# Places of edge groups in a sort block: the segment compare turned so that segments lie on partitions, and the sum moved to the matmul engine

## The reference: what is computed

```python
xn = layernorm(x)
h = xn @ W.T + b;  a1, a2 = h @ w_a1.T, h @ w_a2.T
v = leaky_relu(a1[src] + a2[dst])                 # one value an edge
att = exp(v - segment_max(v, src)) / segment_sum  # softmax over the edges of a node
x = x + segment_sum(att * h[dst], src) + linear_attention(xn)
x = x + slice_attention(layernorm(x))             # 8 heads, 64 slices
```

## Time and profile before

| | |
|---|---|
| median of 3 runs | 1682.46 us (1680.82 to 1684.41) |
| the profiled execution's own time | 1682.33 us |
| its span, first to last instruction | 1680.6 us |
| busy over the span | PE 83%, DVE 78%, POOL 66%, ACT 40% |
| mean granted TensorE clock | 0.914 of full speed |
| loop over the 14 blocks of the sort, on DVE | 79 to 366 us |
| last scatter of the sort, on POOL | 384.1 us |

### The profile page before, as it was taken

The page is one execution under the profiler, slowest core; times in us unless marked ns, Lnnn a source line. Parts: engine busy times, 40 slices in busy tenths (PEclk is TensorE's granted clock), DMA queues, the critical chain, the costliest instruction groups (busy, mean ns, idle before and its releaser), DMA issues. The chain is left out here.

```text
span 1680.6 us, 27556 instructions
## 1 busy us (share of the span) xinstructions
PE 1391.1 (83%) x8473; PEld 1102.6 (66%) x8473; DVE 1310.9 (78%) x3978; ACT 665.2 (40%) x1867; POOL 1111.6 (66%) x1196
## 2 busy tenths in 40 slices
PE   5399989984788889888888888888989888886798
PEld 3277767763567777766666666666767666664587
DVE  8999879973588887888888888888787887873244
ACT  0144333420455454555455454455454544531000
POOL 1078888886777777777777777777777777720000
PEclk9699999985799998999999899899998999997599
DMA  9011112113444444444444444444444444512722
GB/s 231 9 58 53 43 41 65 48 37 87 118 124 123 123 125 124 123 123 127 119 123 123 118 122 123 123 122 124 124 121 124 121 121 116 150 51 68 267 74 72
DMA packets 106322, 180.11 MB, mean 107 GB/s; under 512 B 29183, under 2 KB 77694, under 8 KB 106175
## 3 DMA queue, kind: packets, MB, share of 16 engines
q0 software_dynamic: 44384, 113.26, 26.0%
q1 hardware_dynamic: 48277, 44.22, 9.4%
q10 hardware_dynamic: 13514, 20.87, 3.5%
HBM read 142.98 MB, written 35.29 MB: 106 GB/s over the span
## 5 line engine op out<-in xcount | busy, mean ns | idle before, releaser
L1043 POOL DMA_INDIRECT big<-node_table,rest x850 | 826.6, 972 | 245.4 <-issue 231.9
L1114 PE MATMUL psum<-big 128*125 128x257 f32 x1700 | 437.2, 415 | 73.7 <-DVE big L1615 73.7
L1114 PEld LDWEIGHTS psum<-big 128*125 128x125 f32 x1700 | 342.9, 207 | 139.6 <-DVE big L1615 80.5
L1262 ACT ACTIVATE rest<-big,rest 128x125 f32<-128x125 bf16 x850 | 268.3, 490 | 165.8 <-DVE rest L1563 164.7
L1615 DVE TENSOR_SCALAR big<-big,rest 128x125 f32<-128x125 bf16 x850 | 172.8, 293 | 0.0
L327 POOL DMA_INDIRECT edge_groups<-rest x112 | 143.9, 1285 | 27.2 <-issue 21.8
L1570 DVE TENSOR_REDUCE rest<-rest 128x125 f32<-128x2125 f32 x50 | 118.3, 2367 | 32.2 <-ACT rest L1262 32.2
L1253 ACT COPY big<-psum 125x1024 bf16<-125x1024 bf16 x150 | 103.8, 763 | 38.4 <-PE psum L1091 38.4
L1149 PE MATMUL psum<-big 125*128 125x256 f32 x416 | 101.1, 387 | 0.0
L1135 PE MATMUL psum<-rest,big 128*125 128x512 f32 x208 | 99.7, 601 | 0.0
L1759 PE MATMUL psum<-rest,big 128*125 128x256 f32 x400 | 88.7, 384 | 2.0 <-DVE rest L1812 2.0
(11 more groups left out here) (390 smaller groups left out, 2655.0 us busy)
## 6 DMA issues: line engine op xcount, KB each, us to landing
big<-node_table,rest POOLq DMA_INDIRECT x850
slice_weights<-rest ACTq DMA_DIRECT2D x52, 252.0 KB
big<-slice_weights SPq DMA_DIRECT2D x25, 252.0 KB, 7.4
big<-slice_weights ACTq DMA_DIRECT2D x25, 252.0 KB, 6.9
node_table<-big SPq DMA_DIRECT2D x50, 126.0 KB
normalised_turned<-big SPq DMA_DIRECT2D x50, 125.0 KB
rest<-normalised_turned SPq DMA_DIRECT2D x50, 125.0 KB, 2.5
out_dram<-rest SPq DMA_DIRECT2D x50, 125.0 KB
```

What stands on the lines that cost most here:

```text
L1043: pool.indirect_dma_start(Gt[:, u, q * TW:(q + 1) * TW], None, table, bass.IndirectOffsetOnAxis(ap=item[:, u, 2 * q:2 * q + 1], axis=0)).t ...
L1114: mm = pe.matmul(bank[bAgg][0:R, 0:D + 1], P[:, u, q, :], Gt[:, u, q * TW:q * TW + D + 1], start=q == 0, stop=q == Q - 1)
L1262: act.activation(V[:, :, q], O[:, u, q, 0:R], ACT.Copy, scale=score[:, u, q:q + 1]).then_inc(s_v, 1)
```

## The change

The compare is turned around. The 51 entries now lie on partitions, and the 1024 group numbers along the free axis.

- Once, ahead of the loop: PE transposes the two halves of `starts` (`turn_starts`), ACT copies each block's origins and jumps out of PSUM as columns of 51 partitions, and POOL makes the row of group numbers (an iota of 512 int32 on 51 partitions and its copy to f16), shifts the origins for the second half of the numbers, and splits the jumps into two bf16 parts.
- For each block: DVE compares the 512 numbers of each half with that block's origin of the partition (`groups_reached`, two `tensor_scalar` with f16 in and bf16 out, 51 x 512, the origin being a column operand). It does so one block ahead, and for block 0 just before its first `choose`.
- PE multiplies: for each of the 8 columns of groups, the 51 x 128 piece of the compare is the weight and the two jump parts are the moving columns (`group_jumps`, 8 bf16 matmuls of 2 columns). That gives 128 x 8 x 2 in PSUM.
- DVE adds the two parts (`tensor_reduce`, 128 x 16 out of PSUM), and the old last addition to int32 stays.

`group_jumps(n+1)` stands where `block_starts(n+1)` stood in PE's queue; `group_jumps(0)` stands behind `ranks(3)`, ahead of the loop. Tensors of the first stage are laid over each other in another way to make room.

```diff
+                    pool.iota(group_row_i, [[1, GC * 64]], base=0, channel_multiplier=0).then_inc(masks, 1)
+                    pool.wait_ge(masks, 9)
+                    pool.wait_ge(table_ready, 1)
+                    pool.tensor_copy(group_row, group_row_i).then_inc(masks, 1)
+                    pool.wait_ge(table_part, 6)
+                    pool.tensor_scalar(start_col[:, 1, :], start_col[:, 0, :], -GC * 64.0, None, ALU.add).then_inc(masks, 1)
+                    pool.tensor_copy(jump_parts[:, :, 0], jump_col).then_inc(masks, 1)
+                    pool.wait_ge(masks, 12)
+                    pool.tensor_tensor(jump_parts[:, :, 1], jump_col, jump_parts[:, :, 0], ALU.subtract).then_inc(masks, 1)
...
-                    def block_starts(n):
-                        at = STARTS_AT + 2 * (T + 1) * (n % 2)
-                        pe.matmul(bank[1][:, at:at + 2 * (T + 1)], ident[0:NS, SPB * n:SPB * n + 1].to_broadcast([NS, 128]),
-                                  starts.rearrange("s a t -> s (a t)"), start=True, stop=True).then_inc(starts_psum, 1)
+                    def turn_starts():
+                        pe.transpose(bank[1][0:T + 1, TURNED_AT:TURNED_AT + NS], starts[:, 0, :], ident[0:NS, 0:NS])
+                        pe.transpose(bank[1][0:T + 1, TURNED_AT + NS:TURNED_AT + 2 * NS], starts[:, 1, :], ident[0:NS, 0:NS]
+                                     ).then_inc(starts_psum, 1)
+
+                    def group_jumps(n):
+                        at = STARTS_AT + 2 * GC * (n % 2)
+                        pe.wait_ge(segs, max(3 * n + 1, 2))
+                        for c in range(GC):
+                            mm = pe.matmul(bank[1][:, at + 2 * c:at + 2 * c + 2], reached[:, c // 4, c % 4 * 128:(c % 4 + 1) * 128],
+                                           jump_parts[:, n, :], start=True, stop=True)
+                        mm.then_inc(starts_psum, 1)
...
                     for g in range(2, GPB):
                         ranks(g)
+                    pe.wait_ge(masks, 13)
+                    group_jumps(0)
...
+                    act.wait_ge(starts_psum, 1)
+                    act.copy(start_col[:, 0, :], by_block[:, 0, :, 0]).then_inc(table_part, 1)
+                    act.copy(jump_col, by_block[:, 1, :, 0]).then_inc(table_part, 1)
...
+                    def groups_reached(k):
+                        for h in range(2):
+                            dve.tensor_scalar(reached[:, h, :], group_row, start_col[:, h, k:k + 1], None, ALU.is_ge
+                                              ).then_inc(segs, 1)
...
-                        dve.wait_ge(starts_psum, k + 1)
+                        dve.wait_ge(starts_psum, k + 2)
+                        if k + 1 < NB:
+                            groups_reached(k + 1)
...
-                        dve.tensor_tensor(seg, bank[1][:, at:at + w].unsqueeze(1).to_broadcast([128, GC, w]),
-                                          group_id.unsqueeze(2).to_broadcast([128, GC, w]), ALU.is_le).then_inc(segs, 1)
-                        dve.wait_ge(segs, 3 * k + 1)
-                        dve.tensor_tensor(seg, seg, bank[1][:, at + w:at + 2 * w].unsqueeze(1).to_broadcast([128, GC, w]),
-                                          ALU.mult).then_inc(segs, 1)
-                        dve.wait_ge(segs, 3 * k + 2)
-                        dve.tensor_reduce(seg_sum, seg, AX, ALU.add).then_inc(segs, 1)
-                        dve.wait_ge(segs, 3 * k + 3)
+                        dve.tensor_reduce(seg_sum, bank[1][:, at:at + 2 * GC].rearrange("p (c w) -> p c w", w=2), AX,
+                                          ALU.add).then_inc(segs, 1)
+                        dve.wait_ge(segs, min(3 * k + 5, 3 * NB))
                         dve.tensor_tensor(slot_buf[:, u], seg_sum, group_id, ALU.add).then_inc(slots_ready, 1)
...
                     normalisers()
+                    dve.wait_ge(masks, 13)
+                    groups_reached(0)
                     for g in range(GPB):
                         choose(g)
```

More of the change, by code:

```diff
@@ L142, in bass_gps @@
             key_iota = a.take(128, 128, dtype=F16)
-            iota_i = a.take(128, 128, dtype=I32)
             group_id = a.take(128, GC)
@@ L151, in bass_gps @@
             scal = a.take(1, 4)
-            before = a.take(128, 128)
+            before_at = a.at
+            before, iota_i = a.take(128, 128), a.take(128, 128, dtype=I32)
+            group_row = Arena(rest, before_at, a.at).take(T + 1, GC * 64, dtype=F16)
             item_cmp, item_col = a.take(128, T), a.take(128, 1)
@@ L162, in bass_gps @@
             v2i, v2h = a.take(128, 64, dtype=I32), a.take(128, 64, dtype=I32)
-            seg = a.take(128, GC, T + 1)
+            reached_at = a.at
+            reached = a.take(T + 1, 2, GC * 64, dtype=BF16)
+            group_row_i = Arena(rest, reached_at, a.at).take(T + 1, GC * 64, dtype=I32)
+            start_col, jump_col = a.take(T + 1, 2, NB), a.take(T + 1, NB)
+            jump_parts = a.take(T + 1, NB, 2, dtype=BF16)
             seg_sum = a.take(128, GC)
@@ L199, in bass_gps @@
             hot_done, counted, summed = sem("hot_done"), sem("counted"), sem("block_sums")
-            masks, coded, csum_made, first_made = sem("masks"), sem("coded"), sem("csum_made"), sem("first_made")
+            masks, coded, csum_made, first_made = sem("masks_and_columns"), sem("coded"), sem("csum_made"), sem("first_made")
             table_part, offsets_made, table_ready, starts_psum = sem("table_part"), sem("offsets_made"), sem("table_ready"), sem("starts_psum")
@@ L219, in bass_gps @@
             wa, gb, ba = b.take(128, DC, 2), b.take(128, DC), b.take(128, 2)
-            STARTS_AT, ROW_STEPS = 256, 10
+            TURNED_AT, STARTS_AT, ROW_STEPS = 256, 384, 10
             UNITS = [[] for _ in range(NB)]
@@ L494, in _ @@
                     pe.wait_ge(table_ready, 1)
-                    block_starts(0)
+                    turn_starts()
                     items()
@@ L507, in _ @@
                             pe.wait_ge(moved_made, 3 * (2 * n + 1))
-                            block_starts(n + 1)
+                            group_jumps(n + 1)
                         put(n, 0)
@@ L567, in _ @@
                     assert len(loads) == 12
+                    by_block = bank[1][0:T + 1, TURNED_AT:TURNED_AT + 2 * NS].rearrange("t (a b s) -> t a b s", a=2, s=SPB)
+                    act.wait_ge(starts_psum, 1)
+                    act.copy(start_col[:, 0, :], by_block[:, 0, :, 0]).then_inc(table_part, 1)
+                    act.copy(jump_col, by_block[:, 1, :, 0]).then_inc(table_part, 1)
                     act.wait_ge(prep_psum, 2)
@@ L760, in unpack @@
                         dve.tensor_tensor(edge_buf[:, u, :, 0], v2h, bank[1][:, 128 * h:128 * h + 64], ALU.add).then_inc(edges_ready, 1)
+                    def groups_reached(k):
+                        for h in range(2):
+                            dve.tensor_scalar(reached[:, h, :], group_row, start_col[:, h, k:k + 1], None, ALU.is_ge
+                                              ).then_inc(segs, 1)
                     def places_of_groups(k):
-                        u, at = k % SLOTS, STARTS_AT + 2 * (T + 1) * (k % 2)
-                        w = T + 1
-                        dve.wait_ge(starts_psum, k + 1)
+                        u, at = k % SLOTS, STARTS_AT + 2 * GC * (k % 2)
+                        dve.wait_ge(starts_psum, k + 2)
+                        if k + 1 < NB:
+                            groups_reached(k + 1)
                         if k >= SLOTS:
```

## The result

The changed kernel takes 1672.95 us in the median (1666.29 to 1674.01, 6 runs), the kernel before beside it 1683.6 (1680.82 to 1687.12, 6 runs). The ratio is 0.9934 (0.9916 to 0.9953): 11 us faster, where I had forecast no change and a range from 1675 up. The profiled execution took 1674.01 us, its span is 1672.2.

What follows compares the result with a forecast made beforehand. The prediction took POOL's unbroken queue to bound the sort. From the profiled 1682.3 us, -0.4 for the loop's start and +1.8 for the lock gave 1683.7, forecast as 1683.5, range 1675 to 1687.5.

Steps and rivals of the forecast that it cites:

- Nothing moves in the other stages: Outside the sort's stage: the change was to alter no time there, as no DMA is added.
- Its 71 us of excess stay: POOL in the sort: 71 of 282 us lost beside DVE's f16 operations were to remain, those operations being as many.
- rival B: POOL in the sort: 5 to 10% of the 71 us excess goes, 3.5 to 7 us, giving 1677; chance 0.10.
- The start of the loop: First compare +0.55 us on DVE, block 0 then gains 0.9; POOL's unbroken queue begins earlier, net -0.4 us.
- my lower bound: DVE's new compares: 0.30 us each for 512 elements, at twice the pace of f32.
- my 0.6 to 1.0: DVE's step in each block: the us it was to gain from the change.
- 8 to 13: DVE's two waits for others in the sort, 12.8 us before, were to rise by this many us.
- The lock: DVE's new compares shutting POOL out: 0.15 us for each of twelve pairs, +1.8 us.
- Rival A: DVE sets the sort's pace after all, so its saved time counts: 11 us less, 1671; chance 0.17.
- the last line of my sum: Whole kernel: 1682.3 - 0.4 + 1.8 = 1683.7, that execution 0.1 us below the runs' median; forecast 1683.5.

Runs made afterwards that it cites:

- e_one_cast: The kernel before with one more instruction on POOL, a cast of 128 x 8 int32 to f16 into scratch, without a wait: ratio 0.9965 (0.9951 to 0.9978).
- e_prep_dve: The changed kernel with POOL's new instructions, all but the iota, moved to DVE ahead of its loop: ratio 0.9989 (0.9977 to 1.0001), median 1680.31 us.
- e_more_dve: The changed kernel with three more DVE operations a block (compare, multiplication, reduce of 408 elements, into scratch): ratio 0.9976 (0.9965 to 0.9988).

## Why the prediction was wrong

*"Nothing moves in the other stages"* is the step that failed, and the larger part of the 11 us. Each gather became 7 to 9 ns shorter, 6 to 8 us in 850 of them, and each scatter 9 to 10 ns at its shortest, 1 us in 112. I had counted POOL's five new instructions as run with POOL idle, costing nothing; they didn't cost but paid, through what comes long after them. Shown by `e_one_cast` (5.9 us from one cast alone) and, in the shortest gather and the time, by `e_prep_dve`. No row of the kernel before could have told it. But the earlier trace rows did say that anything that touches the 850 gathers back to back counts in full, and I asked only what was added to them.

*"Its 71 us of excess stay"* failed too. POOL's unbroken stretch, with the same instructions in it, is 4 us shorter on the mean of the four traces with the new step (3.8 in the first pair, 6.0 in the second). The number of f16 operations had stayed, as I said; what POOL lost beside them had not. That is rival B, given 0.10, at the lower end of its 3.5 to 7 us. Half of it went to the later start: 2 us are left at the last scatter, and by `e_prep_dve` some 2 us in the time.

*The start of the loop* was forecast 0.4 us earlier and came later. In the timelines POOL's wait for unit 4 ends at 105.51 us in the changed kernel and at 103.61 in the kernel before:

```profile
105.51 1.36 POOL L353 TENSOR_TENSOR big<-rest 125x256 f32<-125x256 f32 x1 [4.96 <-ACT rest L627]
```

```profile
103.61 1.91 POOL L339 TENSOR_TENSOR big<-rest 125x256 f32<-125x256 f32 x1 [4.97 <-ACT rest L598]
```

The wait is still 4.96 us long, so it hid nothing of PE's delay: units 0 to 3 stand in PE's queue ahead of `put(0, 1)` and unit 4, and whatever delays them delays it. Of the 1.9 us, 0.53 are the first pair, 0.44 `group_jumps(0)` in PE's queue, and 0.7 come from elsewhere: DVE waited for x before its statistics, 1.80 us in the first trace of the changed kernel and 0.73 in this one.

```profile
47.41 16.43 DVE L837 BATCH_NORM_STATS2 rest<-X 125x6 f32<-125x256 f32 x50 [0.73 <-DMA X<-in_x_dram]
```

All seven traces with the new step have such a wait, of 0.5 to 1.8 us, and two of the 13 with the old one; why is open. DVE, level with the kernel before at its first f16 operation (82.29 against 82.20), then waited 2.27 us in block 1, by the order of the queues for the put that stood behind those units; the view names no releaser. POOL's unbroken stretch is 274.6 us against 280.5 in this pair; the gain at the end is 1.9 less than that.

*What held.* The pair, undisturbed, ran at my lower bound, 0.30 us each, which is where the Trainium skill's "VectorE: DVE Perf Modes", section "The perf-mode tier table", puts a 16-bit `tensor_scalar` in SBUF; the trace agrees. The step saved 1.1 us in block 0 and some 0.7 on the mean, within my 0.6 to 1.0; POOL waited for nobody in the loop; DVE's waits rose, by 5 us in the first pair of traces and 4 in the second, not 8 to 13; the first trace's last scatter was within 3 us. The lock has a price, of 0.2 to 0.3 us a pair by estimate, in place of 0.15. The Trainium skill's rule of the shared port pair ("SBUF — State Buffer", section "Who interferes with whom") names who locks out whom, and that agrees with it in kind. By the same rule DVE operations with at most one input in SBUF, outside the 2-port modes, don't contend with GpSimd. The three added in `e_more_dve` are such, and they didn't slow down themselves; yet POOL's stretch got 5 us longer with them, so their effect is indirect. Rival A, that DVE sets the pace, had the right total by another way: a us of DVE's time is worth 0.2 to 0.3, not 1. And the last line of my sum is off by itself: 1683.7 and the 0.1 us to the median make 1683.8, not 1683.5, which changes nothing.

*What stays open.* How a cast shortens the gathers. How the 11 us divide exactly: one cast alone 5.9 us (3.7 to 8.3) and the step alone 2 us (0 to 4) make 8, and the changed kernel has 11 (8 to 14). And the prices of the step don't close: 13 blocks with 0.7 to 1.1 us saved, at 0.2 to 0.3 us per us, are 2 to 4 us, and 12 pairs at 0.2 to 0.3 for the lock take 2 to 4 back, while POOL's stretch fell by 4 on the mean, 2 to 6 by the trace. Either DVE's time is not worth the same per us when it is taken away as when it is added, or the spread hides it; no run decides. And the second stage began 5.9 us after the last scatter in both traces of the changed kernel, 7.5 and 8.0 in the kernel before; the control, the kernel before unchanged, had 5.9 as well, so that isn't the change's.

## What to carry to other kernels

When one queue issues hundreds of equal instructions back to back, compare the shortest and the median of that instruction between two traces before looking for the time anywhere else: nanoseconds times the count were more here than the step that was rewritten. Where two engines exclude each other, "this queue never waits, so the other's time is free" is too strict: its own durations have the other's load in them. To size such a thing, take the whole unbroken stretch in several traces, not the mean of one instruction in two. Change one part at a time also where a part "costs nothing": a test with one cast alone gave more than half of the gain.

## What the runs showed of the hardware

- POOL's indirect DMAs depend on what POOL has run before. In six traces on ordinary chips of kernels without a cast, an addition of a constant or a subtraction to bf16 on POOL the shortest gather was 949 ns (952 in a seventh), in all 13 with one of them 942 or 945, and the shortest scatter 963 to 967 against 954 to 957. Five memsets, waits, an iota of 51 x 512 and another layout don't do it; one cast of 128 x 8 some 350 us ahead of the first gather does. By what path is not known.
- A `tensor_scalar` with f16 in, bf16 out and a column operand, 51 x 512 in SBUF, took 0.30 us undisturbed and 0.43 to 0.45 on the mean of 28 beside a busy POOL.
- 26 us more of DVE operations that ran undisturbed themselves made POOL's stretch in the sort, 277 us without them, 5 us longer (one trace), without a wait of POOL's for another engine in between.
- Eight bf16 matmuls with 51 x 128 weights and two columns took 0.3 us ahead of the loop, from 79.37 to the next matmul at 79.67 in the changed kernel's second trace, where I had counted 0.98; the granted clock there was 0.50, the lower level of 1.2 GHz. From the matmul ahead of them, at 78.94, to the one behind them it is 0.73 us where two neighbours are 0.29 apart, so they cost PE's queue 0.44.
